# Cross attention scores: one fp32 product, or two fp32r products with split operands

## The reference, cut to what matters

```python
q = _split_heads(query @ q_w + q_b, B)      # 16 heads of 16 numbers
k = _split_heads(key @ k_w + k_b, B)
v = _split_heads(value @ v_w + v_b, B)
scores = jnp.einsum('bhqd,bhkd->bhqk', q, k) * SCALE
attn = jax.nn.softmax(scores, axis=-1)
out = jnp.einsum('bhqk,bhkd->bhqd', attn, v)
x = _layernorm(x + out @ o_w + o_b)
```

## Time and profile before

| | us |
|---|---|
| median of three runs | 971.71 |
| lowest, highest | 969.20, 977.56 |
| the profiled execution's own time | 980.14 |
| its span | 978.3 |
| PE busy | 870.4 |
| DVE busy | 605.2 |
| ACT busy | 453.0 |
| POOL busy | 345.7 |

### The profile page before, as it was taken

The page is one execution under the profiler, slowest core; times in us unless marked ns, Lnnn a source line. Parts: engine busy times, 40 slices in busy tenths (PEclk is TensorE's granted clock), DMA queues, the critical chain, the costliest instruction groups (busy, mean ns, idle before and its releaser), DMA issues.

```text
span 978.3 us, 18379 instructions
## 1 busy us (share of the span) xinstructions
PE 870.4 (89%) x6875; PEld 654.3 (67%) x6875; DVE 605.2 (62%) x1410; ACT 453.0 (46%) x845; POOL 345.7 (35%) x336
## 2 busy tenths in 40 slices
PE   7799789789999987998889888979997999999994
PEld 5577566667777765786556555656785777777774
DVE  5799797566889888432557777774462343333255
ACT  5788656446677766342144544445331322222221
POOL 9422200123557566312001343223540242222684
PEclk9999999778999997998799999999999999999998
DMA  5699769897455432124991222002302222221421
GB/s 168 202 269 281 203 153 250 296 240 172 109 119 120 76 76 78 32 86 165 388 338 42 63 63 88 12 24 80 100 23 83 66 60 60 66 66 50 151 65 64
DMA packets 144468, 123.52 MB, mean 126 GB/s; under 512 B 89790, under 2 KB 126590, under 8 KB 143102
## 3 DMA queue, kind: packets, MB, share of 16 engines
q1 hardware_dynamic: 140974, 112.98, 41.0%
q0 software_dynamic: 3408, 9.38, 2.6%
HBM read 74.04 MB, written 48.29 MB: 125 GB/s over the span
## 4 chain that ended last, share of the span: by engine, by line
PE 60%; DVE 14%; ACT 10%; POOL 7%; issue 4%; DMA 3%; SPq 1%; POOLq 0%; DVEq 0%; ACTq 0%; another core or an unknown queue 0%
PE ps L2513 10%; PE ps L1919 6%; PE ps L2528 5%; DVE cross_room L1952 4%; PE ps L1859 3%; PE ps L2377 3%; PE ps L1352 3%; PE ps L666 3%; PE ps L1620 3%; POOL hank L345 2%; PE ps L1981 2%; POOL kept L2660 2%; PE ps L2390 2%; PE ps L423 2%; DMA hank<-rt_dram 2%
## 5 line engine op out<-in xcount | busy, mean ns | idle before, releaser
L1997 ACT ACTIVATE cross_room<-ps 128x1024 f32<-128x1024 f32 x64 | 65.5, 1023 | 99.1 <-PE ps L1923 96.9
L1952 DVE TENSOR_REDUCE cross_room<-ps 128x4 f32<-128x1024 f32 x64 | 78.1, 1224 | 39.3 <-PE ps L1919 38.5
L2513 PE MATMUL ps<-wr,xbT 128*128 x312 | 99.0, 459 | 1.8 <-ACT xbT L2549 1.8
L1919 PE MATMUL ps<-kept,cross_room 32*128 32x256 f32 x512 | 74.1, 411 | 21.7 <-DVE cross_room L1952 18.8
L2602 POOL DMA_INDIRECT y_dram<-yb,dest_row x39 | 37.5, 961 | 134.6 <-DVE dest_row L2578 130.4
L1320 POOL TENSOR_TENSOR st<-st,exponent 128x20 f32<-128x20 f32 x16 | 56.9, 3554 | 64.7 <-DVE st L1295 63.4
L2513 PEld LDWEIGHTS ps<-wr,xbT 128*128 128x128 f32 x312 | 58.8, 189 | 29.5 <-issue 2.5
L1923 PE MATMUL ps<-cross_room,kept 32*128 32x256 f32 x512 | 75.3, 413 | 0.0
L1919 PEld LDWEIGHTS ps<-kept,cross_room 32*128 32x128 f32 x512 | 47.1, 190 | 39.7 <-issue 21.7
L550 DVE SCALAR_TENSOR_TENSOR room<-room 128x256 f32<-128x256 f32 x144 | 58.4, 480 | 11.4 <-ACT room L499 11.4
L2587 DVE TENSOR_TENSOR cross_room<-cross_room,ps 128x352 f32<-128x352 f32 x39 | 20.3, 521 | 58.6 <-PE ps L2513 57.1
(11 more groups left out here) (353 smaller groups left out, 2243.2 us busy)
## 6 DMA issues: line engine op xcount, KB each, us to landing
xs_dram<-params SPq DMA_DIRECT2D x17, 1040.0 KB, 17.9
room<-in_gW SPq DMA_DIRECT2D x8, 1280.0 KB, 7.7
tok_dram<-room SPq DMA_DIRECT2D x8, 768.0 KB, 6.4
fir_dram<-room SPq DMA_DIRECT2D x6, 1024.0 KB, 7.3
paths<-fir_dram SPq DMA_DIRECT2D x48, 128.0 KB, 3.7
xb<-xs_dram SPq DMA_DIRECT2D x39, 130.0 KB, 2.3
hank<-rt_dram SPq DMA_DIRECT2D x8, 512.0 KB, 8.1
yr<-y_dram SPq DMA_DIRECT2D x16, 256.0 KB, 3.2
```

Source lines behind the costliest of these rows:

```text
L1919: m1 = nc.tensor.matmul(ps[:, c, t * T:(t + 1) * T], strips(qS[b % 3], g, c)[:, t * P:(t + 1) * P], kS(b, g)[c * CH:(c + 1) * CH], start=T ...
L1952: V.tensor_reduce(mx[:, :, g, XD + 2 * h * CH:XD + (2 * h + 1) * CH + 1:CH].rearrange("p t c -> p c t"), ps[:, pair(h), :].rearrange("p c ...
L1997: S.activation(pT[g % 2][:, pair(h)].rearrange("p c k t -> p (c k t)"), ps[:, pair(h), :].rearrange("p c n -> p (c n)"), ACT.Exp).then_inc ...
L2513: m = nc.tensor.matmul(ps[:, 2 * (j % 2) + half, 0:FF], xbT[j % 2][:, k, :], wr[:, bass.ds(e, 1), k, half, :].rearrange("p e n -> p (e n)" ...
```

## The change

- Queries and keys take all 32 rows of a strip. The weights of both projections are written twice, into rows 0 to 15 and 16 to 31 (`pool_cross_parameters`), the biases are loaded twice.
- Each score product becomes two fp32r matmuls into the same PSUM: part A, query's rounded value in both halves of the strip (`qA`) against key's rounded value in the lower and key's rest in the upper half (`kA`); part B, query's rest in the lower half and the maximum in row 16 (`qB`) against the key in the lower half and a one in row 16 (`kB`).
- ACT makes qA and, in fp32, the masked query `q_rest` (four instructions for a half of the groups); DVE makes qB from the two with one scalar_tensor_tensor of 128x512, and its two evictions are gone.
- POOL splits the keys of the next batch (`pool_keys`, six instructions of 128x512 per batch), ahead of its values copy; those of batch 0 come first of all in the phase.
- Four masks are made by four small DVE instructions in the phase before; four memsets and four additions on POOL are gone there, four more scalings added.
- The buffers for qB, kA and q_rest lie in the room of experts 3 to 7 of `wr`, whose ten loads are now issued after the last slot (`EARLY = 3`).

The core of the diff:

```diff
+        qA = [nc.alloc_sbuf_tensor_at(f"qA{i}", [P, XG, T], F32R, ...) for i in range(3)]
...
+        def pool_keys(b):
+            pool.wait_ge(s.p2_made, SLOTS * (b - 2))
+            for half in range(KT):
+                k, high = env.kS_half(b, half), halves(kA[b % 3], half)
+                pool.in_turn()
+                G.tensor_scalar(high, k, env.upper, 0.0, ALU.mult, ALU.add).then_inc(*pool.tick(s.keys))
+                pool.in_turn()
+                G.tensor_tensor(high, k, high, ALU.subtract).then_inc(*pool.tick(s.keys))
+                pool.in_turn()
+                G.tensor_scalar(env.x2T[half][:, :, b * T:(b + 1) * T], k, env.lower, env.max_row, ALU.mult,
+                                ALU.add).then_inc(*pool.tick(s.keys))
...
+        pool_keys(0)
         blank = views(env.params, 0, BLANKS * XW, "p (n w) -> p n w", n=BLANKS)
         pool.in_turn()
         G.memset(blank, 0.0).then_inc(*pool.tick(s.blank))
...
+            act.wait_ge(s.p2_made, SLOTS * (b - 2))
+            for half in range(2):
+                yield
+                act.wait_ge(s.q_made, 2 * b + half + 1)
+                for g in range(2 * half, 2 * half + 2):
+                    q = bank(f"q{half}", b)[:, g % 2 * T:(g % 2 + 1) * T]
+                    S.activation(qA[b % 3][:, g, :], q, ACT.Identity, bias=bq[:, g:g + 1]).then_inc(*s.q_evicted.up())
+                    m = S.activation(q_rest[b % 3][:, g, :], q, ACT.Identity, bias=env.bq_lower[:, g:g + 1], scale=env.lower)
+                m.then_inc(*out_of(f"q{half}", b).up())
+                yield
 
         def dve_queries(b):
             yield
             yield
-            dve.wait_ge(s.p2_made, SLOTS * (b - 2))
             for half in range(2):
                 yield
-                dve.wait_ge(s.q_made, 2 * b + half + 1)
-                for g in range(2):
-                    m = V.tensor_scalar(qS[b % 3][:, 2 * half + g, :], bank(f"q{half}", b)[:, g * T:(g + 1) * T],
-                                        bq[:, 2 * half + g:2 * half + g + 1], None, ALU.add)
-                m.then_inc(*out_of(f"q{half}", b).up())
+                copied(dve, f"q{half}", b)
+                dve.wait_ge(s.q_evicted, 4 * b + 2 * half + 2)
+                V.scalar_tensor_tensor(out=halves(qB[b % 3], half), in0=halves(qA[b % 3], half), scalar=env.minus_lower,
+                                       in1=halves(q_rest[b % 3], half), op0=ALU.mult, op1=ALU.add).then_inc(*s.q_ready.up())
                 yield
 
         def pool_values(b):
+            if b + 1 < B:
+                pool_keys(b + 1)
             pool.wait_ge(s.pv_made, XG * (b - 1))
...
             for t in range(TT):
-                if b < B:
-                    for c in range(2 * h, 2 * h + 2):
-                        m1 = nc.tensor.matmul(ps[:, c, t * T:(t + 1) * T], strips(qS[b % 3], g, c)[:, t * P:(t + 1) * P],
-                                              kS(b, g)[c * CH:(c + 1) * CH], start=True, stop=True)
...
+                for part, q in enumerate((qA, qB)):
+                    if b < B:
+                        for c in range(2 * h, 2 * h + 2):
+                            k = strips(kA[b % 3], g, c) if part == 0 else kB(b, g)[c * CH:(c + 1) * CH]
+                            m1 = nc.tensor.matmul(ps[:, c, t * T:(t + 1) * T], strips(q[b % 3], g, c)[:, t * P:(t + 1) * P], k,
+                                                  start=(part == 0), stop=(part == 1))
...
+            for e in range(EARLY, NE):
+                sp_routed_up(e)
```

More of the change, by code:

```diff
@@ L800, in place_tokens_kept @@
     env.kS = lambda b, g: turned[g // KT][:, g % KT, b * T:(b + 1) * T]
+    env.kS_half = lambda b, half: turned[half][:, :, b * T:(b + 1) * T]
     env.xin = views(env.kept, 3 * n_all, n_x, "p (t d) -> p t d", 4, t=TT)
@@ L1684 @@
 BLANKS = 4
+EARLY = 3
 PARTS = ((0, 0), (0, 1), (1, 0))
@@ L1767, in phase_cross, with kB, halves @@
         at += 2 * NCH * TT * T
-        qS = views(room, at, XG * T, "p (g t) -> p g t", 3, g=XG)
+        n_strips, spare = XG * T, EARLY * KT * 2 * FF
+        qA = [nc.alloc_sbuf_tensor_at(f"qA{i}", [P, XG, T], F32R, offset=env.cross_base + 4 * (at + i * n_strips)) for i in range(3)]
+        qB, kA = ([nc.alloc_sbuf_tensor_at(f"{n}{i}", [P, XG, T], F32R, offset=env.wr_base + 4 * (spare + (3 * j + i) * n_strips))
+                   for i in range(3)] for j, n in enumerate(("qB", "kA")))
+        q_rest = views(env.wr[:].rearrange("p e k j n -> p (e k j n)"), spare, n_strips, "p (g t) -> p g t", 3, g=XG)
         at += 3 * XG * T
+        def kB(b, g):
+            return env.x2T[g // KT][:, g % KT, b * T:(b + 1) * T]
+        def halves(t, half):
+            return t[:, KT * half:KT * (half + 1), :]
         vv = views(room, at, TT * XH * CH, "p (t h d) -> p t h d", 2, t=TT, h=XH)
@@ L1903, in pe_scores @@
             if b < B:
-                copied(pe, f"q{g // 2}", b)
+                pe.wait_ge(s.keys, 6 * b + 3 * (g // KT) + 3)
+                pe.wait_ge(s.q_ready, 2 * b + g // 2 + 1)
                 if b >= 1:
@@ L1916, in pe_scores @@
             for t in range(TT):
-                if b < B:
-                    for c in range(2 * h, 2 * h + 2):
-                        m1 = nc.tensor.matmul(ps[:, c, t * T:(t + 1) * T], strips(qS[b % 3], g, c)[:, t * P:(t + 1) * P],
-                                              kS(b, g)[c * CH:(c + 1) * CH], start=True, stop=True)
-                if b >= 1:
-                    for c in range(2 - 2 * h, 4 - 2 * h):
-                        m2 = nc.tensor.matmul(ps[:, c, t * T:(t + 1) * T], kS(b - 1, g)[c * CH:(c + 1) * CH, t * P:(t + 1) * P],
-                                              strips(qS[(b - 1) % 3], g, c), start=True, stop=True)
+                for part, q in enumerate((qA, qB)):
[4 more added lines that the diff above has]
+                                                  start=(part == 0), stop=(part == 1))
+                    if b >= 1:
+                        for c in range(2 - 2 * h, 4 - 2 * h):
+                            k = strips(kA[(b - 1) % 3], g, c) if part == 0 else kB(b - 1, g)[c * CH:(c + 1) * CH]
+                            m2 = nc.tensor.matmul(ps[:, c, t * T:(t + 1) * T], k[:, t * P:(t + 1) * P], strips(q[(b - 1) % 3], g, c),
+                                                  start=(part == 0), stop=(part == 1))
             if b < B:
@@ L2269, in phase_cross @@
         SHARED = 5
-        sp_before = {0: sp_blank} | {e + 2: lambda e=e: sp_weights(e) for e in range(NE)} | {B + 2: sp_last}
+        sp_before = {0: sp_blank} | {e + 2: lambda e=e: sp_weights(e) for e in range(EARLY)} | {B + 2: sp_last}
         weave([sp_queries, idle, idle, idle, idle], B, sp_before)
```

51 lines of the change are left out of this document (28 added, 23 removed).

## The result

The change made the kernel slower: 996.1 us in the median of four runs (989.61 to 999.41) against 973.41, a ratio of 1.022 with a 95% interval of 1.0175 to 1.0266. In five more rounds on another chip it was 1000.63 against 978.16, 1.0235 (1.0183 to 1.0287). The forecast was 977.2 with 951 to 997 as its range.

The account below looks back on a forecast made before the run. A step was taken to alternate between PE and DVE, so PE savings pay only on some legs. Query and PE legs +2.0, POOL's split +5.4 and edges -1.9 gave +5.5 us: 977.2 against 971.7, range 951 to 997.

Parts of the forecast that it names:

- the side that had 0.35: Whole kernel: slower by more than 1% than the kernel before, chance 0.35.
- POOL at every turn: Rival, cross attention: POOL's key split blocks DVE's small instructions at every turn, 19 us more, 996 us; chance 0.17.
- the clock: Rival, cross attention: idle query legs bring PE to 1.2 GHz, 18 us in three steps, 995 us; chance 0.1.
- The likeliest case: Whole kernel: the forecast itself, 977.2 us, own range 965 to 985; chance 0.43.
- The slot on PE: Score matmuls: fp32r groups start 0.12 us apart instead of 0.215, 0.38 us less per slot.
- The queries' path: Legs r3 to r4 and r5 to r6: DVE waits for ACT's four evictions; each becomes 3.76 us, +0.76 and +1.10.
- POOL's split: Leg r0 to r2: small DVE instructions wait out POOL's key instructions, 0.9 us per step, +5.4 us.
- The gain on the other PE legs: Legs r2 to r3, r4 to r5 and r7 to r0: each 0.38 us shorter per step.
- The edges: Start +1.6, first step +1.3, step without queries -1.9, last slots -2.3, and smaller terms: -1.9 us in all.
- The loads after the last slot: Ten loads issued after the last slot arrive before their first reader: zero, at most 20 us.
- the hidden path: Rival, cross attention: the queries' path is hidden and POOL doesn't block, 960 us, or 944; chance 0.27.
- serial strips: Rival, score matmuls: strips don't run together in fp32r, +1.06 us per slot, 1048 us; chance 0.03.

Follow-up runs that it names:

- e1: Changed kernel with ACT's query evictions moved behind the exponent and DVE's scalar_tensor_tensor behind the maximum: 987.77 us, ratio 1.0161; again 980.50 us, 1.0079.
- e2: Changed kernel without POOL's key split (one-element memsets instead, both parts read the once-rounded keys): 998.66 us, ratio 1.0256 to the kernel before.
- e5: Changed kernel with the key split moved to slot r3 and batch 0's keys split on DVE, queries left early: 1004.69 us, ratio 1.0264.
- e8: Changed kernel with only batch 0's key split moved from POOL to DVE: 986.41 us, ratio 1.0180 to the kernel before.
- e6: Changed kernel with queries late and batch 0's keys on DVE, key split left ahead of POOL's values copy: 981.33 us, ratio 1.0024.
- e3: Kernel before with each score product made as two fp32r passes of the same operands, nothing split: 967.57 us, ratio 0.9909.

## Why the forecast was right or wrong

The time lies in the range, 0.9 us under its upper end, and on the side that had 0.35, not on the likeliest. That it is inside is partly luck: the upper end came from two rivals at 996 and 995 us, POOL at every turn and the clock, and neither cost what it was priced at. The likeliest case was short by 17 us. The forecast's sum against the mean of two traces each:

| us | forecast | measured |
|---|---|---|
| start | +1.6 | +4.7 |
| first step | +1.3 | +4.0 |
| six steps, with the four slots at 1.2 GHz | +6.3 | +9.0 |
| the step without queries | -1.9 | +0.5 |
| last slots | -2.3 | -1.4 |
| sum in the cross attention | +5.0 | +16.8 |

- **The slot on PE**: right. 0.12 us a group; 0.41 us less on r7 to r0 (3.32 to 2.91) for the 0.38 taken, and r4 to r5 the same wherever the clock was full. Strips do run together in fp32r.
- **The queries' path**: right in mechanism and size, 3.92 for 3.76. ACT's masked eviction takes 0.565 us, not the 0.469 of the row without a mask. In six steps the two query legs grew by 13.2 us for the 11.2 forecast. This is the largest part of the loss. e1 shows that it is the order on the two lists that costs, not the instructions.
- **POOL's split**: right in mechanism, too high in size. The small DVE instructions do wait, and step 3 has 0.85 us for the 0.9, but step 2 has nothing, and over seven steps e2 without the split is 1.8 us shorter in r0 to r2, for the 5.4 forecast for six. That e2's seven steps are no shorter is the clock's doing as far as the traces show: PE's legs behind took it back.
- **The gain on the other PE legs**: failed. In six steps r2 to r3, r4 to r5 and r7 to r0 were to give 6.8 us and gave 3.0, since r4 to r5 grew by 1.2 where 2.3 should have gone. That is the clock, which the forecast had as a rival of its own at 0.1 (995 us) instead of a term of every case: 51 and 58 us at 1.2 GHz in the change against 17 and 20, and 58, 55 and 44 in e2, e5 and e8, the others with early queries, but 17 to 41 in the six traces with late ones. In r4 to r5 it is clearest: two or three steps of each of the five traces with early queries have the lower clock there, and none of the nine others. That the idle query legs bring the falls is the reading of this order, not shown by a run that changes the clock alone.
- **The edges**: failed, and here lies most of the miss in the cross attention, 9.1 of 11.8 us. The counts end 10.0 us behind DVE's first instruction, where the forecast has 8.4: the six key instructions took 7.0 us and not 5.5, the first of them 1.79. That is 1.6 of the 3.1 us missed at the start; the rest is that the forecast was made from the first trace before, whose start had a fall of the clock, and the second trace starts 3.0 us sooner. In the first step the two scalar_tensor_tensor wait for POOL's locks too (1.58 and 1.14 us for 0.75), which the term of 1.3 left out, and it has 11 us at 1.2 GHz, where the two traces before have 0.8 and none: a slot with query matmuls behind it took 4.03 us instead of 2.99, and 2.59 in e8 at the full clock. The step without queries has the leg r5 to r6 at 3.74 in one trace and falls of the clock in the other.
- **The loads after the last slot**: right, nothing. From the last slot to the end it is 303.0 and 301.4 us before, 305.0 and 301.6 after.
- **The rivals**: the hidden path is refuted by e1, POOL at every turn by e6 (19 us expected, at most 5 found), serial strips by the 0.12. Of the clock's rival the falls came, as far as r4 to r5 shows them at some 4 us for the 18 priced; that its 995 us lies next to the measured 996 is a coincidence, since most of the loss is in other terms.

The phases ahead of the cross attention took 453.1 and 443.7 us in the kernel before, 453.6 and 458.1 in the change, and 455.9 in e3, which has the phases of the kernel before. The last 55 us of them, behind the last of the change's work there, take 55.1 to 55.2 us in all five traces, and the four mask instructions of DVE take 0.65 us together. The short 443.7 has 37 us at 1.2 GHz in these phases, the other four 55 to 68. So the spread between traces is larger than any price of the change that could be read from them; whether its work there costs more than the 0.5 us forecast, and where the 6 us outside the cross attention lie, stays open.

## What to carry to other kernels

When an eviction moves to another engine, ask what stands behind its consumer in that engine's list: here nobody needed the operand for half a step, and one or two rounds later the same instructions took their 1.3 us off each of two legs and put 0.2 us a step on another (r6 to r7). Work put at the head of a phase on an idle engine must be checked for what already stands there and who waits for it. And look at the clock of the work behind a new wait of TensorE: here the leg behind a wait of 1.3 us took 1.3 us longer in three of seven steps. That the wait brings the fall is not shown.

## What the runs showed beyond that

In steps 5 to 7, r0 to r1 took either 2.3 to 2.7 us or 3.6 to 4.1, in either kernel and in two runs of the same one. The second trace of the changed kernel in the slow form, in step 6:

```profile
628.34 0.27 PE L1963 MATMUL ps<-x2Thi,qB 32*128 32x256 f32 x1
629.13 0.96 POOL L2250 DMA_INDIRECT xs_dram<-cy,c_slot  x1 [0.30 <-issue]
630.05 1.23 DVE L1997 TENSOR_REDUCE cross_room<-ps 128x4 f32<-128x1024 f32 x1 [3.19 <-remote]
```

PE's last score matmul starts at 628.34, the maximum that waits for it 1.7 us later, where it was 0.32 in the same step of the first trace. It comes in all three steps of an execution or in none, 3.3 to 5.5 us in r0 to r1, of which r1 to r2 gives a part back (r0 to r2 differs by 2.5 to 3.7 us). The four scatter DMAs of POOL stand beside it, but at the same places in the fast form too, so they alone don't explain it; its cause is open. The first trace of the change is in the fast form and the first of the kernel before in the slow one, so these two alone would show too small a loss (12.0 us; like with like it is 15.5 and 18.1).
